# All four engines between two scans in a newly written order, with the next batch's transposes and the first mixer blocks inside the scan

## The reference

```python
# mixer, per batch; DI = 1024 channels, 16 states
x, z = in_proj(norm(x));  x = silu(causal_conv4(x))
dt, B, C = x_proj(x)
delta = softplus(dt_proj(dt) + bias)
h = h * exp(delta * A) + (delta * x) * B        # over 512 steps, for each channel and state
y = (h * C).sum(states) + x * D
out = out_proj(y * silu(z))
# MLP: twice (gate_up 512 -> 2 x 256, down 256 -> 512)
s = sqrt(max|x| over rows / max|w| over rows)   # per column
x_q = round(x / s / x_scale);  w_q = round(w * s / w_scale)   # scales: row maxima / 127
h = x_q @ w_q.T * x_scale * w_scale.T
# experts
out = sum over the top 2 of prob * w2(silu(w1 x) * w3 x) + sigmoid(x g) * shared(x)
```

## Time and profile before

| what | us |
|---|---|
| median of 3 runs (1992.75 to 1994.79) | 1993.51 |
| the profiled execution | 1994.25 |
| its span, first to last instruction | 1991.7 |
| phase 1 of batch 0 | 0 to 133 |
| scan 0 (no experts beside it) | 133 to 356 |
| between scans 0 and 1 | 356 to 528.6 |
| scan 1 | 528.6 to 805 |
| between scans 1 and 2 | 805 to 983 |
| scan 2 | 983 to 1259 |
| between scans 2 and 3 | 1259 to 1437 |
| scan 3 | 1437 to 1709 |
| MLP of batch 3 | 1709 to 1803 |
| experts of batch 3 | 1803 to 1991.7 |

### The profile page before, as it was taken

The page is one execution under the profiler, slowest core; times in us unless marked ns, Lnnn a source line. Parts: engine busy times, 40 slices in busy tenths (PEclk is TensorE's granted clock), DMA queues, the critical chain, the costliest instruction groups (busy, mean ns, idle before and its releaser), DMA issues.

```text
span 1991.7 us, 19125 instructions
## 1 busy us (share of the span) xinstructions
PE 1477.2 (74%) x5200; PEld 828.5 (42%) x5208; DVE 1454.0 (73%) x2349; ACT 779.1 (39%) x1312; POOL 1081.7 (54%) x675
## 2 busy tenths in 40 slices
PE   6755567985578898976478898976487988647873
PEld 2221222432345564433244564433254664336662
DVE  2359999656698999664698999664698999674111
ACT  3553343246323554235423555235423555031221
POOL 0269899103659888202658888312558988311001
PEclk9877778987689999987699999987788999967997
DMA  2252001311334663412424664402333774412795
GB/s 95 76 197 99 0 1 55 99 65 64 137 107 137 211 218 132 149 48 74 161 89 143 205 214 132 174 26 81 132 117 122 216 223 127 143 59 80 242 300 181
DMA packets 99018, 255.26 MB, mean 128 GB/s; under 512 B 11489, under 2 KB 11617, under 8 KB 93793
## 3 DMA queue, kind: packets, MB, share of 16 engines
q1 hardware_dynamic: 91680, 233.08, 35.3%
q0 software_dynamic: 5120, 16.78, 2.5%
q10 hardware_dynamic: 2112, 4.19, 0.6%
HBM read 211.02 MB, written 42.99 MB: 128 GB/s over the span
## 4 chain that ended last, share of the span: by engine, by line
PE 41%; DVE 20%; issue 16%; POOL 11%; ACT 6%; DMA 4%; SPq 1%; DVEq 0%; POOLq 0%; ACTq 0%
DVE bank L938 6%; PE bank L1478 6%; PE bank L1383 6%; POOL work L556 5%; PE bank L1581 5%; PE bank L1393 5%; DMA ew_up<-in_exp_w 4%; PE bank L1424 3%; PE bank L1430 2%; PE bank L1431 2%; PE bank L1502 2%; DVE work L948 2%; PE bank L1401 2%; POOL CB L519 2%; DVE pairs L948 2%
## 5 line engine op out<-in xcount | busy, mean ns | idle before, releaser
L556 POOL TENSOR_TENSOR work<-du,BB 128x1024 f32<-128x1024 f32 x256 | 603.9, 2365 | 4.6 <-DVE bank L938 4.2
L938 DVE TENSOR_TENSOR_SCAN bank<-bank,work 128x512 f32<-128x512 f32 x448 | 543.1, 1220 | 72.1 <-ACT bank L714 52.7
L714 ACT ACTIVATE bank<-delta,A_sb 128x512 f32<-128x512 f32 x512 | 351.0, 690 | 577.2 <-DVE pairs L948 339.2
L1478 PEld LDWEIGHTS bank<-xT,ew_up 128*128 128x128 f32 x1472 | 193.2, 196 | 102.7 <-issue 77.6
L1478 PE MATMUL bank<-xT,ew_up 128*128 128x128 f32 x1472 | 202.1, 282 | 34.6 <-DMA ew_up<-in_exp_w 20.6
L1393 PE MATMUL bank<-xT,wst 128*128 128x512 f32 x256 | 133.2, 674 | 101.5 <-ACT zg L664 101.5
L948 DVE TENSOR_TENSOR pairs<-bank,CB 128x512 f32<-128x512 f32 x256 | 172.5, 674 | 10.3 <-PE bank L1424 10.3
L1502 PE MATMUL bank<-ew_dn,etm 128*128 128x512 f32 x184 | 104.2, 650 | 36.6 <-ACT xT L750 36.5
L564 POOL TENSOR_TENSOR work<-work 128x512 f32<-128x512 f32 x64 | 80.9, 1264 | 92.4 <-DVE work L948 92.4
L948 DVE TENSOR_TENSOR work<-bank,CB 128x512 f32<-128x512 f32 x192 | 128.8, 671 | 0.0
L1393 PEld LDWEIGHTS bank<-xT,wst 128*128 128x128 f32 x256 | 54.8, 219 | 172.7 <-ACT zg L664 106.5
(11 more groups left out here) (187 smaller groups left out, 2535.1 us busy)
## 6 DMA issues: line engine op xcount, KB each, us to landing
ew_up<-in_exp_w SPq DMA_DIRECT2D x124, 512.0 KB, 3.8
ew_dn<-in_exp_w SPq DMA_DIRECT2D x124, 256.0 KB, 4.2
hm<-xs_dram SPq DMA_DIRECT2D x92, 256.0 KB, 4.6
ys_dram<-xT SPq DMA_DIRECT2D x92, 256.0 KB, 4.5
wst<-in_w_in SPq DMA_DIRECT2D x64, 256.0 KB, 2.7
BB<-bc_dram SPq DMA_DIRECT2D x16, 1024.0 KB, 5.0
CB<-bc_dram SPq DMA_DIRECT2D x16, 1024.0 KB, 7.0
wst<-in_out_w SPq DMA_DIRECT2D x32, 256.0 KB, 2.7
```

What stands on the lines that cost most here:

```text
L556: nc.gpsimd.tensor_tensor(dBu[:, k % CHUNK_SLOTS, :, :], du[:, j % 2:j % 2 + 1, :].broadcast_to([P, 2, T]), BB[:, n0:n0 + 2, :], ALU.mult) ...
L714: nc.scalar.activation(R[q % RING][:, :], delta[:, j, :], ACT.Exp, scale=A_sb[:, j, n:n + 1]).then_inc(S["da_ready"], 1)
L938: V.tensor_tensor_scan(prod[c % (2 * PAIR_SLOTS)] if on_pool(c) else R[q % RING][:, :], R[q % RING][:, :], dBu[:, c // 2 % CHUNK_SLOTS, c ...
L1478: ins = mm(gu_bank(v)[:, part * n:(part + 1) * n], ew_up[:, q % UP_RING, part * D + k * P:part * D + (k + 1) * P], rhs, start=(k == 0), st ...
```

## The change

What each engine computes stays nearly as it is; what changes is where it stands.

- `phase1` is replaced by three written-out orders per engine: `first` for batch 0, `between` for the three stages between scans, `last` for batch 3. Quantisation steps are cut smaller (`smooth`, `diag(side)`, `scale`, `maxima(side)`, `integers(side)`, `transposed(side)`, `column_scales(m, layer)`) so that other work fits between.
- In scan b the four `head` transposes of batch b + 1 go to p = 104, 108, 109, 110, into banks 0 and 1, with ScalarE's copies one position later. To free xT for this, the experts' gathered and output rows live in x3T.
- Mixer blocks 0 to 3 stand at p = 111, 112, 115, 116, one output bank at a time; blocks 4 to 6 at p = 117, 119, 121. Block 7 stays behind the scan, now behind xi 0.
- GpSimd makes the first du and dBu chunk ahead of the second group's sums. ScalarE makes the first three decays ahead of the second group's logarithms. VectorE's second `softplus` group stands at p = 1 of the scan, and the first product waits for it.
- The column maxima of the first weights stand behind the scan's last product. The weights' DMAs get a semaphore each, and the last out-projection block is loaded ahead of x and the down weights.

```diff
-OUT_AT = 113
+HEAD_AT = (104, 108, 109, 110)
+OUT_BANKS_AT = (111, 112, 115, 116)
+OUT_FIRST = 4
+OUT_AT = (117, 119, 121)
...
-        xsT = [xT[:, i, :].rearrange("p (k t) -> p k t", k=KD) for i in range(2)]
-        ys = [xT[:, 2 + i, :] for i in range(2)]
+        xsT = [x3T[:, i, :].rearrange("p (k t) -> p k t", k=KD) for i in range(2)]
+        ys = [x3T[:, 2 + i, :] for i in range(2)]
...
@@ SyncE
                 load_gate_up(b)
                 if b + 1 < B:
                     weights("xi", b + 1, 0, 1)
+                weights("o", b, NBLK - 1, NBLK)
                 load_res(b)
                 load_mlp_down(b)
-                weights("o", b, NBLK - 1, NBLK)
...
@@ GpSimd
                     for i in range(4):
                         softplus_less(a, i)
+                    du_block(a, 0)
+                    chunk(a, 0)
                 if m is not None:
                     norm(2 * m + 1)
...
@@ ScalarE, head
-                if a > 1 and t == 0:
-                    sc.wait_ge(S["gu_done"], VISITS * (a - 1))
-                    for s in range(2):
-                        sc.wait_ge(ys_out[s], 16 * ring_uses(a - 1, s))
+                if a > 1:
+                    sc.wait_ge(S["route_done"], 2 * (a - 1))
...
@@ VectorE, the scan
+                    if c == 0:
+                        ve.wait_ge(S["sp_err_ready"], NBLK * (b + 1))
...
+                    if scan and p == 1:
+                        for i in range(4, 8):
+                            softplus(b, i)
...
+                    if scan and p == UNITS + 1:
+                        column_scales(b, 0)
...
@@ TensorE, the scan
-                    for k in range(NBLK - 1):
-                        if scan and p == OUT_AT + 2 * k:
-                            mixer_out(b, k)
+                    if scan:
+                        for t in range(TT):
+                            if b + 1 < B and p == HEAD_AT[t]:
+                                head(b + 1, t)
+                            if p == OUT_BANKS_AT[t]:
+                                for k in range(OUT_FIRST):
+                                    mixer_part(b, k, t)
+                        for k in range(OUT_FIRST, NBLK - 1):
+                            if p == OUT_AT[k - OUT_FIRST]:
+                                mixer_out(b, k)
...
@@ TensorE, between two scans (the other engines have a list of this kind too)
+            def between(a, m):
+
+                xi(a, 0)
+                mixer_out(m, NBLK - 1)
+                xi(a, 1)
+                bc_dt(a, 0)
+                xi(a, 2)
+                xi(a, 3)
+                norm_transposes(2 * m, x1n, acc, "xn_ready", "tr_done")
...
+                xi(a, 7)
+                z(a, 0)
+                z(a, 1)
...
+                linear(m, 0)
+                dl(a, 0)
+                z(a, 2)
+                dl(a, 1)
+                z(a, 3)
+                gated_rows(m)
...
+                linear(m, 1)
+                z(a, 7)
+                dl(a, 6)
+                dl(a, 7)
```

776 lines of the change are left out of this document (440 added, 336 removed).

## The result

| | us | 
|---|---|
| kernel before, median of 4 runs (1991.09 to 1994.79) | 1993.13 |
| changed kernel, median of 4 runs (1896.77 to 1901.42) | 1899.80 |
| ratio, with 95% interval | 0.953 (0.9514 to 0.9547) |
| forecast (range) | 1878.5 (1856 to 1924) |

The profiled execution took 1898.37 us, its span is 1896.5, and TensorE's mean granted clock over it is 0.884. The kernel is 4.7% faster, 93 us where 115 were forecast. The gain is a fifth short of the forecast, and most of the difference lies between the scans. The median is inside the narrower band of 1869 to 1900 by 0.2 us, with two runs on either side of its edge; that it came out inside is luck.

What follows compares the result with a forecast made beforehand. VectorE bounds the scans; between them no engine is full and chains of waits bind. Gains of 103 (three stages between scans), 5 (scan ends), 4 (first stage) and 3 (last) sum to 115 us, giving 1878.5 us, range 1856 to 1924.

Steps and rivals of the forecast that it cites:

- the two faults of order: Between scans: late weight row leaves GpSimd idle 23.15 us; z blocks behind ScalarE's softplus leave TensorE idle 21.07 us.
- Part 1: Between scans, up to the first linear: weights scaled about E+40, TensorE the limit, linear ending E+64 instead of E+78.5.
- E: End of the scan's last sum on TensorE, from which the milestones of a stage between scans are counted.
- Part 2: Between scans, first to second linear: weights scaled by E+87, linear ending E+105; 41 us for what took 49.
- to this I add 3 us for contention: Between scans: allowance for VectorE's first L919 group beside GpSimd's sums, 5.4 us at most, nothing at least.
- Part 3: Second linear to scan: unit 0 at E+121, 16 us behind the linear instead of 40; unit 4 at E+135.
- fall into this hole and are free: Scan start: VectorE's four softplus products, about 2.5 us, fit while it waits for GpSimd's late chunks, at no cost.
- The scan's end: TensorE starts remaining mixer work and sums right after its last expert matmul: 1.2 us in each of four scans, 5 together.
- First and last stage: Before scan 0, interleaved z blocks gain 4 us; in the last stage, mainly column maxima gone, 3 us gained.
- (b): Rival: GpSimd's late entry into each scan decides, costing 9 to 13 us in each of four: say 1920; 17 in 100.
- (a): Rival: the walk holds without losses, no contention, three stages gain 4 us more each: 1866; 18 in 100.
- (c): Rival: half the order blocks itself through ScalarE's queue, 18 of each stage's 36 us lost: 1932; 6 in 100.
- (d): Rival: slower, the new order leaves TensorE at half its clock between scans: 2100; 2 in 100.

Runs made afterwards that it cites:

- mixer_old_places: Changed kernel with the seven mixer blocks back at their old places (units 113 to 125), head transposes still inside the scan: 1895.65 us.
- less_between: Changed kernel with GpSimd's four subtractions of the second softplus group split around chunk 2, two before and two after: 1899.78 us.
- logs_first: Changed kernel with ScalarE's second group of logarithms ahead of the scan's first three decays again, instead of behind them: 1900.35 us.
- after_integers: Changed kernel with z 7 ahead of the last integer transposes and GpSimd's first four subtractions held until VectorE's last integers of the second linear: 1892.69 us.

## Why the prediction was right, and where it was too high

- **What bounds the kernel, and the two faults of order.** Right. GpSimd's 23.15 us before the first weights and TensorE's 21.07 us before the z blocks were the gain: undoing the one costs 24 us, the other 39. The rest (head transposes inside the scan, first decays early) was not tried singly; if the two add, 30 of the 93 us remain without an experiment of their own.
- **Part 1, E+64 and E+40.** Right: 63.4 and 41.8 (39.0 in the stage without a combine). TensorE is the limit there, busy 63.40 of 63.40 us, and closely: a weight row 11 us later cost 7.8.
- **Part 2, 41 us.** This step failed: it took 47.4. The walk used durations of instructions that run alone, and "to this I add 3 us for contention" was mis-sized: VectorE's excess in the stage is 15.7 us, some 8 of it ahead of the second linear (110.8 against 102.6 with GpSimd's part taken away). In the terms of the sum 8 us belonged where 3 stood: without them the walk had unit 4 at E+135, and it came at E+143.0. I counted only L919 beside the sums; the products beside the subtractions and the integers (0.89 to 4.09) were not in the sum. The row of L919 was the right evidence, and it should have been applied to every VectorE instruction that GpSimd's sums and subtractions now stand beside.
- **Part 3.** From linear to unit 0 16 us were forecast and 15.9 measured. Unit 4 came 16.3 behind unit 0 where the walk had 14. The four products that "fall into this hole and are free" took 7.54 us, not 2.5, and nearly fill it: VectorE waits 1.73 us for GpSimd there, where 4 to 8 was named as a sign. What ends last is still GpSimd: from its first sum to the end of chunk 2 it takes 16.95 us (915.30 to 932.25), where the walk's five pieces make 14.5 to 15.8. So the products are not free either, as far as they lengthen these; how much of it is theirs the runs don't separate.
- **The scan's end, 5 us.** Gone: 1.1 over four scans (2.1 lost in scan 0, 2.8 gained in scan 2, which is within what scans with the same code differ by). From its last expert matmul to E TensorE takes 41.9 us (747.12 to 788.98) where it took 41.2 (774.21 to 815.4). In the kernel before nothing stands idle between that matmul and E, so there was nothing to start sooner. That the mixer's new places are free was right (`mixer_old_places`).
- **First and last stage.** 2.4 and 4.6 us for 4 and 3, so the last one hides 1.6 us of what the others lack.
- **Rivals.** (b) named the right engine by the wrong mechanism: unit 4 does come 10 us later behind unit 0 than before (16.3 against 6.3), but letting GpSimd enter sooner gave nothing (`less_between`, `logs_first`). What GpSimd costs is VectorE's time, and its own. (a), (c) and (d) did not occur; the clock between scans is 0.89 to 0.90, where above 0.9 was named. The wait at the scan's end is in pieces, as named (2.99, 4.70 and 1.95 us are the largest).

Open: what part of the 10 us by which unit 4 comes later behind unit 0 is contention and what GpSimd's own time; and why scans with experts differ by up to 5 us between kernels with the same code in them (277.6 to 283.0 us from unit 4 to E of scan 1), which hides effects under some 4 us.

## What to carry to other kernels

A written order can be walked from the trace's durations to within 2 us in 90, but VectorE's durations must be those beside GpSimd wherever both have tensor work on SBUF; list what stands beside what before adding up. When such work is moved off the path, look at what it lands on, and at which of the two engines starts first there: here the excess in the middle stage stayed between 15 and 19 us in every order, a start 0.1 us earlier moved 6 us of unit 0 from one engine to the other, and only less work on GpSimd took it away. An idle engine just ahead of a step (TensorE before the last transposes) is the place for the independent block that now stands behind it; that alone gave 12.7 us.

## What the runs showed of the hardware

- Four one-input `tensor_scalar` of VectorE (L983, 128x512 float32) took 1.43 to 1.99 us with GpSimd idle or lightly loaded and 5.70 beside its tensor work; four of 128x256 to bf16 took 0.89 and 4.09. I had expected this of two-input instructions alone.
- GpSimd pays too: four sums or subtractions of 128x512 took 4.94 us at best, 5.8 to 6.2 in most places beside VectorE, 7.92 beside its L987 in `logs_first` and 8.59 in the first stage of `after_integers`; four multiplications 4.93 and 7.74.
- Who pays goes by who starts first. In `after_integers` the same instructions met twice: VectorE 0.04 us ahead, and its four L989 took 2.49 us and GpSimd's first sum 4.03; GpSimd 0.12 us ahead, and the four L989 took 7.86 and its four sums 6.10.
- VectorE's products with one input in PSUM (L1018) took 0.67 to 0.69 us each while GpSimd was at work beside them (at 926.50, 928.23 and 929.95 of the changed kernel's span), so these are not held up.
